# Decoder block: the sums and the outputs of attention's values as one block of TensorE per iteration

## The reference

```python
x = x + attn(layernorm(x))       # 32 heads of 32, 8 groups of keys and values, rope, causal softmax, Wo
x = x + xattn(layernorm(x), ctx) # fake-quantised (0..255) matmul with ctx, 2 x 1024 x 1024
x = x + ffn(layernorm(x))        # Q8.8 fixed-point linear layer with bias

# attn, per batch and head h (kv group h // 4)
scores = q @ k.T / sqrt(32); scores = where(causal, min, scores)
ctx = softmax(scores) @ v;   return ctx @ Wo
```

## Time and profile before

| | |
|---|---|
| median of 3 runs | 471.97 us (469.7 to 473.51) |
| the profiled execution | 474.66 us, of which its span from first to last instruction 472.9 us |
| busy, share of the span | PE 93%, DVE 79%, ACT 63%, POOL 61% |
| length of an iteration of attention, for most G | 13.95 us |
| granted clock of TensorE, mean | 0.992 |

### The profile page before, as it was taken

One profiled execution on the slowest core, in us unless ns is written; L12 is line 12 of the kernel. 1 busy time (PEld: TensorE's weight loads), 2 busy tenths in 40 slices (PEclk: granted clock), 3 DMA queues, 4 the chain that ended last, 5 costly groups with the idle time before them and its releaser, 6 DMA issues.

```text
span 472.9 us, 9689 instructions
## 1 busy us (share of the span) xinstructions
PE 439.0 (93%) x3730; PEld 240.0 (51%) x3730; DVE 375.6 (79%) x961; ACT 299.8 (63%) x302; POOL 287.1 (61%) x157
## 2 busy tenths in 40 slices
PE   0699997999799999999999999999998999899896
PEld 0576454455455555555545555555443444446442
DVE  5799873687789888889878999996296658799775
ACT  4766252041867777977778998889836223797633
POOL 6002463054799999999998888989811970706000
PEclk9999998899999999999999999999999999999999
DMA  8653386522051111011144123333186010000044
GB/s 335 222 205 130 112 262 209 156 107 79 13 169 46 59 58 58 25 46 58 46 131 150 49 89 113 115 114 111 34 286 261 23 46 22 1 1 2 3 178 181
DMA packets 21042, 50.93 MB, mean 108 GB/s; under 512 B 4736, under 2 KB 10112, under 8 KB 19712
## 3 DMA queue, kind: packets, MB, share of 16 engines
q1 hardware_dynamic: 19696, 41.79, 25.7%
q10 hardware_dynamic: 1296, 8.45, 5.2%
HBM read 40.67 MB, written 9.44 MB: 106 GB/s over the span
## 4 chain that ended last, share of the span: by engine, by line
PE 47%; POOL 22%; DVE 17%; DMA 6%; ACT 3%; issue 3%; SPq 1%; ACTq 0%; POOLq 0%; DVEq 0%
PE ps L1466 14%; PE ps L1288 8%; POOL more L1205 6%; PE ps L1617 5%; PE ps L1368 5%; POOL s1reg L1205 4%; POOL wkv L1205 4%; PE ps L1333 4%; DVE stat L769 4%; PE ps L1352 4%; DMA qstack<-in_x 2%; DMA rope_scratch<-s1reg 2%; PE ps L1572 2%; POOL s1reg L1197 2%; POOL s1reg L1201 2%
## 5 line engine op out<-in xcount | busy, mean ns | idle before, releaser
L829 DVE CUSTOM_DVE_ANT_0 ps<-ps,causal 128x512 f32<-128x512 f32 (+3 forms) x256 | 121.0, 511 | 20.4 <-PE ps L1333 17.3
L566 ACT ACTIVATE s1reg<-ps 128x1280 f32<-128x1280 f32 x64 | 78.9, 1233 | 37.0 <-PE ps L1354 36.9
L1288 PE MATMUL ps<-xT,wqx 128*128 128x512 f16 x384 | 97.3, 386 | 0.0
L1466 PE MATMUL ps<-wo_reg,xT 128*128 128x512 f16 x384 | 93.0, 379 | 0.0
L1333 PE MATMUL ps<-kreg,qstack 96*128 96x512 f16 (+3 forms) x256 | 60.7, 302 | 5.2 <-DMA qstack<-rope_scratch 3.3
L1352 PE MATMUL ps<-qstack,kreg 98*128 98x512 f16 (+3 forms) x256 | 57.2, 300 | 1.1 <-ACT s1reg L566 0.9
L1288 PEld LDWEIGHTS ps<-xT,wqx 128*128 128x128 f16 x384 | 37.3, 99 | 38.0 <-issue 3.4
L1186 POOL TENSOR_TENSOR s1reg<-s1reg 128x512 f32<-128x512 f32 x11 | 16.0, 1452 | 65.0 <-DVE s1reg L818 65.0
L1466 PEld LDWEIGHTS ps<-wo_reg,xT 128*128 128x128 f16 x384 | 36.5, 97 | 36.7 <-issue 0.2
L1205 POOL TENSOR_TENSOR s1reg<-s1reg 128x1280 f16<-128x1280 f32 x19 | 49.7, 2627 | 4.9 <-ACT s1reg L572 4.8
L1205 POOL TENSOR_TENSOR wkv<-s1reg,wkv 128x1280 f16<-128x1280 f32 x18 | 47.0, 2625 | 4.6 <-ACT wkv L572 4.6
(11 more groups left out here) (134 smaller groups left out, 924.1 us busy)
## 6 DMA issues: line engine op xcount, KB each, us to landing
s1reg<-in_weights ACTq DMA_DIRECT2D x8, 1024.0 KB, 5.1
s1reg<-in_ctx SPq DMA_DIRECT2D x16, 512.0 KB, 4.2
qstack<-rope_scratch SPq DMA_DIRECT2D x48, 128.0 KB, 2.6
rope_scratch<-s1reg SPq DMA_DIRECT2D x40, 128.0 KB, 2.2
qstack<-in_x SPq DMA_DIRECT2D x8, 512.0 KB, 6.4
s1reg<-in_x SPq DMA_DIRECT2D x16, 256.0 KB, 3.3
out<-s1reg SPq DMA_DIRECT2D x7, 512.0 KB, 3.2
s1reg<-in_L_ffn_weight SPq DMA_DIRECT2D x5, 512.0 KB, 6.6
```

Of the source, the lines that this page charges most:

```text
L566: nc.scalar.activation(ebuf[:, j % 2, :], st_ps[:, 0:SCORES], ACT.Exp, scale=EXP_SCALE, bias=P_LOG_SCALE).then_inc(e_done, 1)
L829: last = nc.vector.tensor_tensor_reduce(part, part, causal[:, T - w:T], 1.0, LOWEST, ALU.add, ALU.max, mt[:, G % 2, h, qt:qt + 1])
L1288: last = mm(out_ap, w(ws, k), xT[:, xs, KT * b + k, :], start=(k == 0 and n == 0), stop=(k == KT - 1 and n == 2))
L1466: last = mm(ps[:, bank, :], xT[:, os, KT * b + k, t], wo_sb[:, ws, 4 * h:4 * h + 4, k, :], start=(k == 0 and n == 0), stop=(k == KT - 1 an ...
```

## The change

The two parts of `values` become one, where the sums were. Its order is now: sums of the high parts, outputs of the high parts times high values, and only then the wait for the low parts and the sums of these, then the two other products of the outputs. The wait for `mrow_ready` moves up with it. Unit 2 and unit 3 come to stand together behind filler 0. VectorE does `heads_norm` at once behind `sums_inverse`, instead of behind unit 2's maxima; in iterations 9 to 14 `wo_add`, which stood ahead of it, comes behind it. In the last iteration the outputs move in the same way, and in the final call the first product of the outputs moves ahead of the sums of the low parts. No instruction is added or taken away.

```diff
@@ VectorE, the loop over G
                 if G:
                     sums_inverse(G - 1)
+                    heads_norm(G - 1)
                 if 1 <= g < KV - 1:
                     wo_add(g - 1, (g - 1) % 2, FILL, 16 * ((g - 1) // 2 + 1))
-                maxes(G, 2, 3)
-                if G:
-                    heads_norm(G - 1)
-                maxes(G, 3, 6)
+                maxes(G, 2, 6)
@@ TensorE
-            def values(G, outputs):
+            def values(G):
...
-                if not outputs:
-                    pe.wait_ge(ph_done, HG * G + HG)
-                    product(DEN, ph, lambda k: ones_h[:, 0:DH], True, False)
-                    for j in range(HG):
-                        pe.wait_ge(pl_done[j], G + 1)
-                    product(DEN, pl, lambda k: ones_h[:, 0:DH], False, True).then_inc(den_done, 1)
-                    return
+                pe.wait_ge(ph_done, HG * G + HG)
+                product(DEN, ph, lambda k: ones_h[:, 0:DH], True, False)
                 pe.wait_ge(mrow_ready, min(G + 2, NG))
                 product(NUM, ph, lambda k: vext[:, k, G, 0:DH], True, False)
+                for j in range(HG):
+                    pe.wait_ge(pl_done[j], G + 1)
+                product(DEN, pl, lambda k: ones_h[:, 0:DH], False, True).then_inc(den_done, 1)
                 product(NUM, ph, lambda k: vext[:, k, G, DH:2 * DH], False, False)
                 product(NUM, pl, lambda k: vext[:, k, G, 0:DH], False, True).then_inc(pv_done, 1)
@@ the loop over G
                 score_units(G, 0, 2)
                 if G:
-                    values(G - 1, False)
+                    values(G - 1)
                 scores_t(G, slot, 1)
                 filler(G, 0)
-                score_units(G, 2, 3)
-                if G:
-                    values(G - 1, True)
-                score_units(G, 3, 4)
+                score_units(G, 2, 4)
                 scores_t(G, slot, 2)
@@ the last iteration
-            values(G - 1, False)
+            values(G - 1)
             scores_t(G, G % KV * HG, 1)
             filler(G, 1)
             filler(G, 2)
-            values(G - 1, True)
             scores_t(G, G % KV * HG, 2)
...
-            values(NG - 1, False)
-            values(NG - 1, True)
+            values(NG - 1)
```

More of the change, by code:

```diff
@@ L1355, in scores_t @@
                 last.then_inc(st_done, 1)
-            def values(G, outputs):
-                if G:
-                    pe.wait_ge(o_norm, G)
-                else:
-                    pe.wait_ge(rope_mul, 12)
+            def values(G):
                 def product(bank, part, weight, first, final):
@@ L1370, in product @@
                     return last
-                if not outputs:
-                    pe.wait_ge(ph_done, HG * G + HG)
-                    product(DEN, ph, lambda k: ones_h[:, 0:DH], True, False)
-                    for j in range(HG):
-                        pe.wait_ge(pl_done[j], G + 1)
-                    product(DEN, pl, lambda k: ones_h[:, 0:DH], False, True).then_inc(den_done, 1)
-                    return
+                if G:
+                    pe.wait_ge(o_norm, G)
+                else:
+                    pe.wait_ge(rope_mul, 12)
+                pe.wait_ge(ph_done, HG * G + HG)
+                product(DEN, ph, lambda k: ones_h[:, 0:DH], True, False)
                 pe.wait_ge(mrow_ready, min(G + 2, NG))
                 product(NUM, ph, lambda k: vext[:, k, G, 0:DH], True, False)
+                for j in range(HG):
+                    pe.wait_ge(pl_done[j], G + 1)
+                product(DEN, pl, lambda k: ones_h[:, 0:DH], False, True).then_inc(den_done, 1)
                 product(NUM, ph, lambda k: vext[:, k, G, DH:2 * DH], False, False)
```

## The result

The changed kernel takes 486.13 us (median of 6 runs, 482.75 to 488.1), the kernel before 472.18 in the same comparison (6 runs, 469.7 to 474.06). The ratio is 1.0287, with a 95% interval of 1.0237 to 1.0337: slower by 11.2 to 15.9 us.

What follows compares the result with a forecast made beforehand. TensorE, busy throughout the 13.95 us iterations, was the bound. Iteration 1 0.34, 2-7 6 x 0.65, 8 1.0, 9 0.78, 10-14 5 x 1.27, 15 -0.20, end 0.55: 12.7 us onto 471.97 gives 484.7, range 481 to 489.

Steps and rivals of the forecast that it cites:

- The two waits: TensorE waits for `st_ps`: `scores_t 2` starts 0.22 us later, `scores_t 3` 0.65 later with rope, 1.27 with `ctx`.
- Fewer crossings: One way into and one out of TensorE's narrow matmuls go away: 0.20 us less work an iteration.
- The larger figure from the Trainium skill's two pages: Estimate that the removed pair of crossings on TensorE would be worth some 0.34 us an iteration.
- The second exp: On ScalarE, the second head's `exp` starts at 5.04 and not 3.44, 1.60 us later, behind the longer block.
- No hole behind `scores_t 3`: TensorE, busy in all of the 13.95 us, had no hole there in which the delay could be given back.
- VectorE at nothing: Both moves of VectorE cost nothing; its busy time is 12.46 and 12.78 us in iterations of 14.6 and 15.2.
- GpSimd at nothing: GpSimd's queue moves with ScalarE's and has 13.82 us of work in 14.6.
- The margin for its second `p_low`: Head 1's `p_low` ends at 10.1, before head 3's `exp` at 10.25 or 10.4: 0.1 to 0.3 us to spare.
- The bounds: Added time in attention of 11.3 to 14.1 us, widened for the spread of runs to 481 to 489 us.
- the last two rivals: A further wait for `p_low` at head 3's `exp`, 490 us, chance 5%; a falling clock, 492 and more, 2%.
- the last rival: TensorE's clock falls: half an iteration at 1.2 GHz costs 7 us a time, 492 us and more; chance 2%.
- The first rival: TensorE stays the bound and fewer crossings pay, with GpSimd's 13.82 us the floor: 1.9 us faster, 470.1; chance 4%.

Runs made afterwards that it cites:

- the added crossing: Kernel before with unit 3 put between the outputs' first and second products, one more way into and out of the narrow matmuls: 477.26 us, ratio 1.0119.
- three-, four- and five-product runs: Kernel before with three products ahead of `scores_t 1`, 474.44 us, or four, 478.6 us; five is the changed kernel, 486.13 us.
- the last experiment: Kernel before with the single block only in iterations 1 to 7, fillers moved to cover its waits, ScalarE's and GpSimd's rope operations early: 472.67 us, ratio 0.9975.
- the run in which it did bound: Changed kernel with ScalarE's `rope_high` and first `ctx` put ahead of the second `exp`: 479.43 us, ratio 1.0177.
- GpSimd's order: Changed kernel with `rope_high` and `ctx` ahead of the second `exp`, plus GpSimd's `rotated_low` ahead of the second `p_low`: 478.42 us, ratio 1.0129.

## Why the prediction was right

The direction, the place and the size came out: forecast 484.7 us in a range of 481 to 489, measured 486.13, and 12.7 us of added time against 12.59 in the profile's stretch and 13.95 in the medians, whose interval (11.2 to 15.9) holds both. The two waits that the working named are the ones that the traces show. One reading beside them was wrong, without a price.

Point by point, with the forecast first:

| iterations | forecast | the profiles |
|---|---|---|
| 1 | 0.34 | 0.34 |
| 2 to 7 | 3.90 | 3.95 |
| 8 | 1.0 | 0.86 |
| 9 | 0.78 | 0.79 |
| 10 to 14 | 6.35 | 6.44 |
| 15 and the end | 0.35 | 0.21 |
| sum | 12.7 | 12.59 |

The iterations are measured from first `exp` to first `exp`. The sum is closer than its parts, which are off by up to 0.14 in both directions.

- *Fewer crossings*: 0.20 an iteration, from the earlier trace rows; the block is 2.84 long (202.65 to 205.49; 2.85 forecast), and the added crossing measured 0.20 to 0.22. The larger figure from the Trainium skill's two pages (TensorEngine Tiling (Array Packing), Key Properties; TensorE: Matmul & The Clock Gate, Single matmul latency) isn't borne out: 0.34 would have put the extra crossing's run at 14.29 before VectorE's 0.1. That a change of the mode costs TensorE a pause at all, this case's rows agree with.
- *The second exp*: 1.59 later; the three-, four- and five-product runs move it in equal steps.
- *The two waits*: `scores_t 2` and `scores_t 3` as in the table of the section on the result. Taking ScalarE's `ctx` and rope out of the path removed the second and left the first.
- *No hole behind `scores_t 3`*: this reading was wrong, and it cost the forecast nothing. The share of busy time hides a wait of 0.17 us at unit 10 (shown above in the last experiment). It wasn't used up by the change, since VectorE's maxima there follow TensorE: from `scores_t 3` to the next `scores_t 0` it is 5.34 us in the changed kernel and 5.33 before.
- *VectorE at nothing*: shown by putting its order back, 0.01 us in the stretch.
- *GpSimd at nothing*: right for the changed kernel. The margin for its second `p_low` held everywhere but in iteration 15, where the fourth `exp` stood idle for 0.35 us for `p_low`, with nothing behind it that the end waits for.
- *What was seen too wide*: the prediction named late units and `p_low` as what would be next, and the maxima's DMA only in front of iteration 9. In the changed kernel this DMA was the nearest of all: SP issued it at 213.47, and from the run in which it did bound (issued at 213.47, `scores_t 0` at 215.93) it takes 2.46 us from issue to use, so it would have allowed a start at 215.93, and TensorE came at 216.06. 0.13 us less in an iteration and it would have been the bound. The changed kernel's own trace agrees: the load for this `scores_t 0` already waits for the DMA, until 215.91, while the matmuls ahead of it still run (`215.91 0.10 PEld L1350 LDWEIGHTS ps<-qstack,kreg 98*128 98x128 f16 x1 [0.18 <-DMA qstack<-mrow]`). That DMA is why the forecast for ScalarE's work ahead of the second `exp` was missed by 3.4 us, of which GpSimd's order gave 2.1 back.
- *The bounds*: the working says that either end takes 2 us more, and adds 2.5 at the upper end. With 2 it would be 488, and the result lies inside either way. The chances of the forecast and the last two rivals add up to 0.92, and 0.91 was given.
- *The clock*: it stayed at 1.00 through the changed kernel's attention, against the last rival. The one fall that a profile of an experiment shows there cost 0.76 us (last section), not the 7 that the rival put on one.

The first rival, with no slower time, needed the third `exp` to be covered. It isn't in the changed kernel; the last experiment's edits make that case true, and then GpSimd's floor, which the rival named, takes the gain away from the fourth iteration on.

## What to carry to other kernels

A block that is moved earlier for TensorE's sake is late work for the engine that it is moved past. Before putting work ahead of a hand-over, take from the trace the slack of the hand-over behind it, the next engine's idle time plus the time that the buffer lies free: up to that the move costs nothing, beyond it 1 to 1, and an engine with 3% of the chain can then set the length. And a saving on an engine that is 100% busy is worth at most the distance to the next engine's busy time (here 13.82 of 13.95, and from the fourth iteration on not even that was reached).

## What was not expected of the hardware

The part ahead of attention took a different time in each profiled execution, with the same instructions: the first `exp` stood between 115.25 us (the changed kernel) and 118.99 (the extra-crossing run). Its granted clock goes with it. Two stretches, of the kernel with the extra crossing and of the changed kernel:

```profile
82.00:95.00 13.00, 13.00 (x52) 5.46 (x51) 8.83 (x16) 0.27 (x1) 0.00 (x0) 0.83 0.52 168
```

```profile
82.00:95.00 13.00, 13.00 (x76) 7.32 (x75) 11.62 (x18) 3.42 (x3) 2.07 (x2) 1.00 0.61 211
```

Behind the same wait for a DMA before 80 us the granted clock was lower for a part of the stretch in the one (0.83 is a mean between its two levels, 1.2 and 2.4 GHz) and full in the other. The two first `exp`s lie 3.74 us apart; how much of this is the clock's wasn't tested. It is more than a quarter of what this change moved, and it is why the spans of two profiles are a poor measure of a change in attention. In attention itself the clock stayed at 1.00 in the changed kernel, with TensorE waiting for 0.4 to 1.1 us at a time.

Once it did fall in attention, in iteration 0 of the four-product run. Two stretches of that run, and for comparison the first of them in the kernel before and what follows it there:

```profile
116.00:119.00 3.00, 1.07 (x8) 0.42 (x6) 2.96 (x8) 2.51 (x2) 1.32 (x2) 1.00 0.13 44
120.00:122.00 2.00, 2.00 (x9) 0.94 (x7) 0.91 (x5) 1.97 (x2) 1.56 (x1) 0.50 0.00 0
```

```profile
118.00:121.00 3.00, 1.07 (x10) 0.48 (x7) 2.95 (x8) 2.31 (x2) 1.16 (x1) 1.00 0.13 44
122.00:124.00 2.00, 1.70 (x14) 0.81 (x11) 1.03 (x5) 1.81 (x2) 1.89 (x1) 1.00 0.00 0
```

In both TensorE is busy for 1.07 of 3 us, by the same wait for VectorE. Behind it the clock fell to 1.2 GHz (0.50) until about 123.4 in the one and stayed at 2.4 GHz in the other. Why it did so in one execution only stays open.
